# Decoder layer on one core: own buffers for the fourth norm and for two residuals, first tokens loaded before the weights, table loads by need, another order in each step

## The reference

```
h  = layer_norm(x, ln1);  xk, xv, xr = mixes of h and of h one token back
k, v = xk @ Wk.T, xv @ Wv.T
x  = x + (sigmoid(xr @ Wr.T) * wkv(k, v)) @ Wo.T          # x1; wkv: three running scans over the tokens
h  = layer_norm(x, ln2);  xk, xr = mixes as above
x  = x + sigmoid(xr @ Wrec.T) * (square(relu(xk @ Wkey.T)) @ Wval.T)      # x2; 256 -> 1024 -> 256
q  = layernorm(x); per token, scores of 16 heads against 16 heads of ctx (16 wide, causal), softmax, times ctx
x  = x + that                                              # x3
p  = layernorm(x) @ U1 @ V1 + b1;  x = x + (gelu(p) @ U2) @ V2 + b2       # rank 64
```

## Time and profile before

| | |
|---|---|
| three runs | 1297.94, 1295.64, 1297.85 us; median 1297.85 |
| profiled execution, its own time | 1296.42 us |
| its span, first to last instruction | 1294.5 us |
| mean granted TensorE clock | 0.933 of full |
| busy | PE 1041.9, DVE 1076.4, ACT 972.5, POOL 870.2 us |

### The profile page before, as it was taken

The page is one execution under the profiler, slowest core; times in us unless marked ns, Lnnn a source line. Parts: engine busy times, 40 slices in busy tenths (PEclk is TensorE's granted clock), DMA queues, the critical chain, the costliest instruction groups (busy, mean ns, idle before and its releaser), DMA issues.

```text
span 1294.5 us, 14561 instructions
## 1 busy us (share of the span) xinstructions
PE 1041.9 (80%) x3584; PEld 586.1 (45%) x3584; DVE 1076.4 (83%) x2172; ACT 972.5 (75%) x2026; POOL 870.2 (67%) x783
## 2 busy tenths in 40 slices
PE   0569596979889697979889797979989797969625
PEld 0236263544536263644636263543637263545302
DVE  2673999998989899998989899999989889858681
ACT  7767678878777778877787778877787877656424
POOL 0110897959586777958686776949686877868590
PEclk9879799999989899999999899999999998979767
DMA  5010010101010010101010010101010000110000
GB/s 179 17 33 16 17 33 16 34 16 50 17 49 1 17 49 16 49 17 49 16 49 0 17 49 16 49 17 49 16 34 16 27 24 16 33 33 17 1 16 17
DMA packets 38964, 38.39 MB, mean 30 GB/s; under 512 B 2932, under 2 KB 38648, under 8 KB 38904
## 3 DMA queue, kind: packets, MB, share of 16 engines
q1 hardware_dynamic: 38904, 37.77, 9.2%
HBM read 29.38 MB, written 8.39 MB: 29 GB/s over the span
## 4 chain that ended last, share of the span: by engine, by line
PE 53%; DVE 23%; ACT 10%; issue 6%; POOL 5%; SPq 1%; DMA 1%; DVEq 0%; ACTq 0%; POOLq 0%
PE bank L795 17%; PE bank L848 15%; PE bank L879 4%; PE bank L872 4%; PE bank L802 4%; PE bank L863 4%; DVE aa L1242 4%; POOL prod L349 3%; DVE stat L1131 3%; ACT n L449 2%; DVE pp L1199 2%; PE bank L891 2%; POOL prod L337 2%; DVE x L1347 1%; DVE o_att L1333 1%
## 5 line engine op out<-in xcount | busy, mean ns | idle before, releaser
L337 POOL TENSOR_TENSOR prod<-q,kv_ctx 128x256 f32<-128x256 f32 (+5 forms) x448 | 370.1, 870 | 223.7 <-ACT q L449 223.7
L349 POOL TENSOR_TENSOR prod<-prob,v_dh 128x256 f32<-128x256 f32 (+3 forms) x256 | 399.1, 1599 | 36.0 <-ACT prob L551 36.0
L795 PE MATMUL bank<-xk,w_key 128*128 128x512 f32 x512 | 236.0, 606 | 16.5 <-DVE xk L1173 16.5
L848 PE MATMUL bank<-w_val,hidden 128*128 128x256 f32 x1024 | 223.6, 379 | 0.0
L848 PEld LDWEIGHTS bank<-w_val,hidden 128*128 128x128 f32 x1024 | 194.6, 190 | 26.5
L1333 DVE TENSOR_REDUCE o_att<-prod 128x64 f32<-128x256 f32 (+3 forms) x256 | 191.1, 807 | 7.8 <-POOL prod L349 7.7
L1301 DVE TENSOR_REDUCE score<-prod 128x16 f32<-128x256 f32 (+5 forms) x448 | 175.8, 466 | 8.7 <-POOL prod L337 8.7
L809 PE MATMUL bank<-ident,n 128*128 128x128 f32 x384 | 58.3, 294 | 126.7 <-ACT n L449 126.7
L795 PEld LDWEIGHTS bank<-xk,w_key 128*128 128x128 f32 x512 | 95.1, 193 | 138.5 <-issue 124.8
L357 POOL TENSOR_TENSOR rr<-rr,bb 128x512 f32<-128x512 f32 x32 | 42.4, 1324 | 129.8 <-DVE bb L1231 129.8
L809 PEld LDWEIGHTS bank<-ident,n 128*128 128x128 f32 x384 | 47.5, 151 | 160.4 <-issue 159.0
(11 more groups left out here) (100 smaller groups left out, 2026.9 us busy)
## 6 DMA issues: line engine op xcount, KB each, us to landing
x_in<-in_x SPq DMA_DIRECT2D x16, 512.0 KB, 3.5
kv_ctx<-in_ctx SPq DMA_DIRECT2D x16, 512.0 KB, 3.8
n<-in_x SPq DMA_DIRECT2D x16, 512.0 KB, 3.5
out<-y_out SPq DMA_DIRECT2D x16, 512.0 KB, 4.5
w_key<-in_wkey SPq DMA_DIRECT2D x1, 1024.0 KB
w_val<-in_wval SPq DMA_DIRECT2D x1, 1024.0 KB
w_k<-in_wk SPq DMA_DIRECT2D x1, 256.0 KB, 2.7
w_v<-in_wv SPq DMA_DIRECT2D x1, 256.0 KB, 3.1
```

The source lines that it names most:

```text
L337: ins = pool.tensor_tensor(o, a, b, ALU.mult)
L349: ins = pool.tensor_tensor(o, ph[:, HB * n:HB * n + HB, 0:keys].unsqueeze(2).to_broadcast(shape), vh[:, :, 0:keys].unsqueeze(1).to_broadca ...
L795: mm = pe.matmul(to[:, :], w[:, fi, P * f:P * f + P], src[:, fi, :], start=(fi == 0), stop=(fi == CH - 1))
L848: mm = pe.matmul(bank[6 + t // 2][:, C * (t % 2):C * (t % 2) + C], hidden[:, j, P * t:P * t + P], w_val[:, j, :], start=(j == 0), stop=(j ...
```

## The change

What it does:

1. n4 has its own buffer. x1 and x3 are two buffers each, by the parity of the group. o_att is gone: `sum_values` and `over_mass` write to x3, and `third_residual` adds x2 to it in place. New waits belong to this: `first_residual` on x2_done of two groups before, `sum_values` on y_done of two groups before, `both_ln` on back_done of the group before.
2. SP issues the load of the first group's tokens before everything else. PE no longer waits for the weights at its start; `project_k` of the first group waits for the first three matrices, `project_o` of the first group for the rest.
3. A table is loaded where `use_table` finds that another one is in, as the program is written out. In steps 3 to 17 this is four times a step as before, in steps 1, 2 and 18 twice, in step 19 once, in steps -2 to 0 not at all: 68 loads for 89.
4. Each engine's order within a step is another one. `project_k(i, 1)` follows `project_k(i, 0)` directly. The lists below give the new orders.

```
-        x1 = sb("x1", [P, TT, C])
+        x1 = [sb(f"x1_{p}", [P, TT, C]) for p in range(2)]
-        o_att = sb("o_att", [P, TT * NH, HD])
-        x3 = sb("x3", [P, TT, C])
-
-        n4 = n2
+        x3 = [sb(f"x3_{p}", [P, TT, C]) for p in range(2)]
+
+        n4 = sb("n4", [P, TT, C])
...
         def _(sp):
+            sp.dma_start(x_in[:, :, :], x_g[0]).then_inc(x_loaded, 16)
             sp.dma_start(vec[:, :], vecs).then_inc(vec_loaded, 16)
...
+            def use_table(name):
+
+                if table[0] != name:
+                    act.preload_act_table_set(name)
+                    table[0] = name
...
-            pe.wait_ge(att_w_loaded, 16 * 3)
-            pe.wait_ge(rest_w_loaded, REST_W)
...
+                if not some(g):
+                    pe.wait_ge(att_w_loaded, 16 * 3)
                 pe.wait_ge(xk_done, upto(g, 2))
                 feature_major(bank[f], f, w_k, xk, k_mm)
...
             def first_residual(g, par, s):
                 dve.wait_ge(wo_mm, upto(g, 2, s + 1))
                 dve.wait_ge(back_done, upto(g, 1))
+                if some(g - 1):
+                    dve.wait_ge(x2_done, upto(g - 2, 2, s + 1))
...
-            def sum_values(g, t, slot):
+            def sum_values(g, par, t, slot):
                 dve.wait_ge(v_prod, upto(g, 4, t + 1))
+                if t == 0 and some(g - 1):
+                    dve.wait_ge(y_done, upto(g - 2, 2))
                 for n, keys, at in V_PARTS:
                     src = prod[slot][:, at:at + HB * HD * keys].rearrange("p (a b) -> p a b", b=keys)
-                    o = o_att[:, NH * t + HB * n:NH * t + HB * n + HB, :].rearrange("p h d -> p (h d)")
+                    o = heads(par, NH * t + HB * n, NH * t + HB * n + HB).rearrange("p h d -> p (h d)")
                     ins = dve.tensor_reduce(o, src, AX.X, ALU.add)
```

POOL's step, whole, as a diff of its order:

```
                 if on(1):
-                    add_bb(i - 1, 0)
-                    add_aa(i - 1, 0)
                     add_aa(i - 1, 1)
-                    add_bb(i - 1, 1)
                 if on(3):
...
                     value_products(i - 3, 3, 1)
+                if on(1):
+                    add_bb(i - 1, 0)
+                    add_bb(i - 1, 1)
                 if on(2):
...
                     score_products(i - 2, p, 1, 1)
+                if on(0):
+                    add_aa(i, 0)
```

More of the change, by code:

```diff
@@ L219, in some, with drive @@
             return not isinstance(g, int) or g > 0
-        def drive(eng, step):
+        def drive(eng, fill, step, drain, enter=None):
             for i in range(-2, LOOP[0]):
-                step(i, i % 2, lambda lag, i=i: 0 <= i - lag < NG)
+                fill(i, i % 2, lambda lag, i=i: 0 <= i - lag < NG)
+            if enter is not None:
+                enter()
             with eng.Fori(LOOP[0], LOOP[1] - 1, 2) as i:
@@ L229, in drive @@
             for i in range(LOOP[1], LAST):
-                step(i, i % 2, lambda lag, i=i: 0 <= i - lag < NG)
+                drain(i, i % 2, lambda lag, i=i: 0 <= i - lag < NG)
         def seqs(t, f):
@@ L296, in step @@
                     store_out(i - 4)
-            drive(sp, step)
+            drive(sp, step, step, step)
             sp.wait_ge(out_stored, 16 * NG)
@@ L395, in step @@
                     score_products(i - 2, p, 1, 1)
-            drive(pool, step)
+                if on(0):
+                    add_aa(i, 0)
+            drive(pool, step, step, step)
         @block.scalar
         def _(act):
-            act.preload_act_table_set(EXP_SET)
+            table = [None]
+            def use_table(name):
+                if table[0] != name:
+                    act.preload_act_table_set(name)
+                    table[0] = name
+            use_table(EXP_SET)
             act.wait_ge(vec_loaded, 16)
@@ L619, in step @@
                     copy_n4T(i - 4, 1)
+                if on(2):
+                    shift_of(2, i - 2)
+                if on(1) or on(4):
+                    use_table(GELU_SET)
+                if on(1):
+                    gate_of_r(i - 1, 0)
+                if on(2):
+                    if on(3):
+                        act.wait_ge(tr2_mm, upto(i - 3, 2))
+                    normalise_2(i - 2, p)
+                if on(4):
+                    copy_pT(i - 4)
+                if on(1):
+                    gate_of_r(i - 1, 1)
                 if on(2):
@@ L779, in step @@
                     att_now(i, 1)
-                act.preload_act_table_set(EXP_SET)
+                if on(2):
+                    gate_of_rec(i - 2, 1)
+                if on(1) or on(0) or on(-1) or on(2):
+                    use_table(EXP_SET)
+                if on(1):
+                    ln_den(i - 1, 0)
+                    inverse_den(i - 1, 0)
                 if on(0):
                     scale_back(i, p)
-            drive(act, step)
+                if on(1):
+                    ln_den(i - 1, 1)
+                    inverse_den(i - 1, 1)
+                if on(-1):
+                    both_ln(i + 1)
+                if on(2):
+                    variance_ln(3, i - 2)
+                    rstd_of(3, i - 2)
+                    shift_of(3, i - 2)
+            drive(act, step, step, step, lambda: use_table(EXP_SET))
         @block.tensor
@@ L828, in project_o @@
             def project_o(g, s):
+                if not some(g):
+                    pe.wait_ge(rest_w_loaded, REST_W)
                 pe.wait_ge(rwkv_done, upto(g, 2))
@@ L1094, in step @@
                     project_k(i, 0)
-            drive(pe, step)
+                if on(0):
+                    if on(2):
+                        pe.wait_ge(relu_done, upto(i - 2, 8))
+                    elif on(4):
+                        pe.wait_ge(y_done, upto(i - 4, 2))
+                    elif on(1):
+                        pe.wait_ge(gnum_done, upto(i - 1, 2))
+                    project_k(i, 1)
+            drive(pe, step, step, step)
         @block.vector
@@ L1371, in step @@
                 if on(2):
+                    add_x_again(i - 2, p)
+                    ffn_before_k(i - 2, 0)
                     ffn_before_k(i - 2, 1)
@@ L1374, in step @@
                     sum_scores(i - 3, 1, 1)
+                    top_scores(i - 3, 0)
+                    shift_scores(i - 3, 0)
+                if on(1):
+                    scan_bb(i - 1, 1)
+                if on(3):
+                    sum_scores(i - 3, 2, 2)
+                    sum_scores(i - 3, 3, 0)
                 if on(2):
```

347 lines of the change are left out of this document (153 added, 194 removed).

## The result

The kernel after takes 1246.2 us (median of 4 runs, 1234.7 to 1257.07) against 1296.74 (median of 4 runs of before). The ratio is 0.9588, interval 0.9508 to 0.9668. Ratios are formed from fast runs alone; slow ones are left out, here that of 1257.07 us, in the experiments among others two of 1841.14 and 1909.75 us at a mean granted clock of 0.56. The forecast was 1265, a ratio of about 0.975. So the direction came as forecast, and the gain was 50.5 us where 31.7 were forecast, 19 us more.

What follows compares the result with a forecast made beforehand. No single engine bounds the kernel; a ring through DVE, PE and ACT does. From 1296.4, less 17.4 (fill), 2, 14 (steady steps) and 1 (drain) gives 1262; plus 1.4 for the median and 1.6 for hand-overs, 1265 us; range 1242 to 1304.

Steps and rivals of the forecast that it cites:

- The fill: Start to first val pass: earlier tokens, fewer table loads and overlap gain 17.4 us, val pass at 96, not 113.15.
- 7.4 from part 2: Start of the fill: issuing the first tokens first brings the first k to 25.7, 7.4 us earlier.
- The steady step: Loop, val pass to val pass: new order takes 71.8 us against 73.07, 14 us gained over 11 steps.
- The early product: DVE's aa scans and bonus products directly together: rv ready at 34 to 35.8, not 40.2, u1 starts at 35.
- the loop's end: End of a loop pass on DVE: 2.53 us of issue stays, every second step, adding 1.2 a step.
- PE's ring: Steady step through PE and ACT: key 0 at 47.2 to 47.4, val pass 23.1 later, giving 70.4 us.
- DVE's: 70.6: Steady step on DVE: 65 us of work plus waits give 70.6; forecast to set the step.
- The buffers, part 1, cost nothing and allow this: Steady step: the added buffers are free and let norm 4 go before norm 2's transposes; otherwise some 2 us wait.
- The port rival: Loop: add_x_again waits out POOL's run, 77.3 us a step, 1324 us in all; chance in most steps 0.17.
- DVE's work alone: Rival, steady state: the counted waits overlap, 69.5 us a step, 1238 us in all; chance 0.10.
- Nothing in the steady state: Rival: ACT hand-overs eat the steady gain, 1277 us; chance 0.27, shared with port in up to half the steps.
- no change: Rival, whole kernel: the fill's gain is given back, as SP's loads hold the pipeline; chance 0.04.

Runs made afterwards that it cites:

- The tokens alone: Kernel before with only the first tokens' load issued first and PE's weight waits moved: 1294.87 us, ratio 0.9997.
- the version without those two stalls: Kernel after with over_mass 0 behind sum_values 3, and add_x_again behind scan_bb 1 only in the written-out last steps: 1233.5 us, ratio 0.9515 to before.
- the kernel with bb 0 ahead: Kernel after with scan_bb 0 back ahead of scan_aa 1 and the second bonus product: 1312.56 us, ratio 1.0103 to before.

## Why the prediction was right, and where it was not

**The fill: the sum right, one term wrongly explained.** First k forecast near 26, at 24.32; first val pass near 96, at 96.91; 17.4 us forecast, 16.2 measured. The closeness is in part luck: up to the first k, to the second, to key 0 and to the val pass 7.4, 5.5, 3.5 and 1.0 were forecast, and 8.8, 5.7, 1.7 and 0.1 came. And the prediction gave "7.4 from part 2" and said of the 21 loads that "only two lie on the path". The tokens alone gave 1.35. Ten loads, 12.9 us of ACT, stood between the early tokens and the first norm; only parts 2 and 3 together give the gain. I had read ACT only from the first norm on, and had not asked what ACT would be doing at 9 us.

**The next two steps:** 2 us forecast, 3.2 measured.

**The steady step: the walk right, several of its numbers too high.** Forecast 71.8, and mean 70.29, or 68.99 without the two long ones. The early product went as forecast (u1 "at 35", at 36.05). The terms that were mis-sized: u1 was taken at 3.68 "as before" and took 1.98: it ended at 38.0 and not 38.8, though it started a microsecond later than forecast, and key 0 is at 46.1 and not 47.3, while key to val came out at 23.1 as forecast; the loop's end was put at 2.53 every second step and measured 0.8; and DVE's waits were put at 4.5 to 5 a step, where the step shown has 1.8 (0.65, 0.78 and 0.36 in its rows), with 67.2 us busy where 65 were taken. PE's ring, 70.4 in the walk less the 1.2 of key 0's start, is 69.2: what the step takes. That this ring sets it more than "DVE's: 70.6" is what more work on PE (nearly all of 3.46 us through) and on DVE (0.45 of 1.2) say; DVE has little slack all the same. The kernel with more work on ACT did not fit in SBUF and has no time, so what ACT holds is open.

**The buffers.** "The buffers, part 1, cost nothing and allow this": no cost of theirs was isolated, and they allow nothing that was measured, as the order runs without them.

**The port rival.** The mechanism held and its place was wrong in the loop. The overlap that the rival asked for was there (479.38 within 475.01 to 488.57), and `add_x_again` got in in all the steady steps. The one that starves is `over_mass` 0, which the prediction did not look at, in 2 steps of 11 at 7.2 us each; and `add_x_again` pays in the last full step, 12.78. With it and the 7.19 in the drain, that step and the drain lose 6.4 us where 1 us of gain was forecast.

**DVE's work alone** (69.5 a step, 1238) was the nearer rival in size: the short steps are just that long, though by the ring of PE.

**Nothing in the steady state, no change:** both wrong; the fill's gain stayed and the mean step is 2.8 us shorter.

Sum by terms, forecast and measured: 17.4 and 16.2; 2 and 3.2; 14 and 33.7 (the step behind the first three, and the eleven); 1 and -6.4. That is 34.4 and 46.7. That the time lies within the stated 1242 to 1304 is in part luck as well: the steady step was mis-sized by more than the total shows, and stalls at instructions that the sum did not charge brought the time back up; the version without those two stalls takes 1233.5, below the range.

What stays open: what decides in a given step whether a DVE instruction gets in. With the same order it did and did not. Where in POOL's running product it starts does not decide it: at 791.95 in after, `over_mass` 0 starts 0.26 us into one and is done in 0.92, and in the kernel with bb 0 ahead, at 545.66, it starts 0.27 us into the same one and takes 8.49.

## What to carry to other kernels

When a load is moved ahead, list what every engine does between the old and the new time of its first user, idle-looking set-up instructions too. A product that another engine waits for goes ahead of a scan that only the next stage needs, and it can be worth more than the scan when the waiting engine's clock falls meanwhile. Keep DVE instructions with two SBUF inputs out of POOL's long unbroken runs, above all at the end where such runs merge: a stall there comes in some steps and not in others and counts as busy time.

## What was not expected of the hardware

- A DVE instruction with two inputs in SBUF can wait out a whole run of POOL instructions, 12.78 us of a run of 22.35, and a similar one gets in at once (0.96, with 20.93 us of a run in view around it).
- The spread of a kernel may be a sign of it. After ran from 1234.7 to 1257.07, the version without its two stalls from 1231.3 to 1234.77. That the stalls make the spread is not shown, as one execution of each was profiled.
- The end of the same loop cost DVE up to 2.8 us in one order of instructions and at most 0.8 in another.
- The same four matrix products took 1.98 us behind a wait of 0.66 or 1.61, and 3.68 or 3.77 behind one of 4.97 or 4.21, at granted clocks of 1.00 and of 0.53 or 0.50. The wait just ahead is not all of it: in before they took 1.95 behind 1.82 (at 508.99) and 3.46 behind 1.73 (at 288.10).
